# Cross attention with row sums on ScalarE, a logarithm in the row of maxima, and projections a batch sooner

## What is computed

```python
qp = q @ Wq.T
k, v = jnp.split(latent_kv @ Wkv_expand.T, 2, axis=-1)
...
scores = jnp.einsum('bhqd,bhkd->bhqk', qh, kh) * inv_sqrt_d
scores = jnp.where(causal, scores, jnp.finfo(scores.dtype).min)
attn = jax.nn.softmax(scores, axis=-1)
out = jnp.einsum('bhqk,bhkd->bhqd', attn, vh)
return out.transpose(0, 2, 1, 3).reshape(b, sq, H) @ Wout.T
```

## Time and profile before

| | us |
|---|---|
| median of 3 runs | 1062.95 |
| lowest and highest | 1061.24, 1067.86 |
| the profiled execution | 1065.82 |
| its span, first to last instruction | 1064.1 |
| cross attention within it | 293.8 to 550.7 |

### The profile page before, as it was taken

The page is one execution under the profiler, slowest core; times in us unless marked ns, Lnnn a source line. Parts: engine busy times, 40 slices in busy tenths (PEclk is TensorE's granted clock), DMA queues, the critical chain, the costliest instruction groups (busy, mean ns, idle before and its releaser), DMA issues. The chain is left out here.

```text
span 1064.1 us, 18069 instructions
## 1 busy us (share of the span) xinstructions
PE 1005.4 (94%) x6352; PEld 857.4 (81%) x6352; DVE 669.4 (63%) x1515; ACT 454.0 (43%) x803; POOL 261.4 (25%) x362
## 2 busy tenths in 40 slices
PE   7899999999979999999979989999999999999996
PEld 5688888888868888887757778989988999778785
DVE  4837546378266677776566837777777775253576
ACT  5523414236125455454534216666665664221210
POOL 4610010103143333333412012312231220503040
PEclk9999999999987999999998989999999999899999
DMA  4503013022786788877622247788778783615042
GB/s 162 194 1 119 0 59 148 0 79 97 210 224 148 218 204 233 232 218 200 212 104 73 82 144 251 246 268 279 236 263 276 253 258 110 221 36 178 19 158 79
DMA packets 87248, 172.79 MB, mean 162 GB/s; under 512 B 8113, under 2 KB 36017, under 8 KB 85393
## 3 DMA queue, kind: packets, MB, share of 16 engines
q1 hardware_dynamic: 81072, 150.21, 45.2%
q0 software_dynamic: 6112, 21.76, 6.2%
HBM read 131.05 MB, written 37.49 MB: 158 GB/s over the span
## 5 line engine op out<-in xcount | busy, mean ns | idle before, releaser
L45 PE MATMUL a_ps_proj<-region_a_rounded,arena 128*128 128x512 f32 x272 | 107.8, 396 | 10.7 <-DVE region_a_rounded L369 6.2
L45 PE MATMUL e_ps_h<-e_x_lo,e_gu_hi 128*128 128x256 f32 (+1 forms) x384 | 110.5, 288 | 3.8 <-DVE e_x_lo L2189 1.3
L962 DVE CUSTOM_DVE_ANT_0 b_dump<-b_ps_s,b_mask 128x128 f32<-128x128 f32 (+1 forms) x256 | 80.3, 353 | 48.5 <-PE b_ps_s L1157 45.3
L46 PE MATMUL e_ps_h<-e_x_hi,e_gu_lo 128*128 128x256 f32 (+1 forms) x384 | 107.5, 280 | 0.0
L47 PE MATMUL e_ps_h<-e_x_hi,e_gu_hi 128*128 128x256 f32 (+1 forms) x384 | 107.4, 280 | 0.0
L46 PE MATMUL a_ps_proj<-region_a_rounded,arena 128*128 128x512 f32 x272 | 106.7, 392 | 0.0
L47 PE MATMUL a_ps_proj<-region_a_rounded,arena 128*128 128x512 f32 x272 | 106.6, 392 | 0.0
L388 DVE SCALAR_TENSOR_TENSOR f_region_b<-a_ps_proj,a_taps,f_region_b 128x510 f32<-128x510 f32 (+2 forms) x96 | 71.7, 746 | 41.0 <-ACT f_region_b L328 38.7
L2195 DVE TENSOR_TENSOR e_gu_lo<-f_region_a,e_gu_hi 128x704 fp32r<-128x704 f32 x92 | 81.2, 886 | 16.6 <-ACT e_gu_hi L2101 16.1
L848 ACT ACTIVATE b_pt<-b_ps_x 128x384 f32<-128x384 f32 x128 | 61.8, 487 | 60.0 <-PE b_ps_x L1181 59.8
L762 POOL TENSOR_SCALAR_AFFINE_SELECT b_pt<-b_pt 128x256 f32<-128x256 f32 x128 | 54.3, 428 | 123.0 <-ACT b_pt L848 122.5
(11 more groups left out here) (418 smaller groups left out, 2665.5 us busy)
## 6 DMA issues: line engine op xcount, KB each, us to landing
f_region_a<-we_gate_up SPq DMA_DIRECT2D x88, 352.0 KB, 5.2
qk_split<-arena SPq DMA_DIRECT2D x24, 512.0 KB, 5.4
y_slots<-f_region_b SPq DMA_DIRECT2D x16, 512.0 KB, 3.7
f_x_next<-x SPq DMA_DIRECT2D x6, 1024.0 KB, 7.4
b_sk<-qk_split SPq DMA_DIRECT2D x24, 256.0 KB, 4.1
b_sq<-qk_split SPq DMA_DIRECT2D x24, 256.0 KB, 5.7
f_region_a<-we_down SPq DMA_DIRECT2D x12, 512.0 KB, 4.4
f_region_b<-we_down SPq DMA_DIRECT2D x11, 512.0 KB, 4.1
```

Of the source, the lines that this page charges most:

```text
L45: pe.matmul(out, a_hi, b_lo, start=first, stop=False)
L46: pe.matmul(out, a_lo, b_hi, start=False, stop=False)
L962: ins = dve.tensor_tensor_reduce(dump[:, n % 2, cols], ps_s[:, n % 2, cols], mask[:, cols], -1.0, 3e38, ALU.add, ALU.min, peak[:, u, k, i: ...
```

## The change

- `attend` has only its second pass; `invert`, `keep`, `spread_out`, `normalize` and `rest`, with their tiles and semaphores, are gone.
- After `maxima`, ACT takes for each head two exponentials of `dump` (128 and 256 columns; scale -1, the maximum as bias) in place, with the row sums in the accumulator output (`totals`), one head behind its `exponent`. `maxima` of a head now waits for the totals of the head two before (it writes the same `dump` buffer). Once per half ACT takes the logarithm of the sums (`logs`), DVE subtracts it from the maxima (`shifts`), and this difference goes into the rows that were those of the maxima. `maxima` scales by `SCALE`, and the row's rounding divides by it.
- ACT's table set is `natural_log_exp_and_others` instead of `exp_and_others`.
- The copies of x, queries and values move from ACT to DVE (those of the first batch's values stay). `attended` reads `ps_o`: ACT rounds directly behind `attend`, DVE subtracts at heads 0 and 1 of the next t, ahead of which POOL's `rest` was at heads 3 and 4.
- `load_peaks` moves from SP to POOL, behind the cut of head 4 of either half; the transposition moves to head 3 of either half.
- `projected(t)` is t + 3: batch 3 at t = 0, up to batch 7 at t = 4, none from t = 5. The context has three buffers (`CB`), and `split_stored` is one semaphore for each half.

```diff
...
+        CB = GB + 1
...
+        total = sb("total", [P, 2, BT, UH])
+        log_total = sb("log_total", [P, 2, BT, UH])
+        shift = sb("shift", [P, 2, BT, UH])
...
-            return {-1: GB, 0: B}.get(t, t + 2)
+            return t + 3
...
                 if b >= GB:
-                    sp.wait_ge(split_stored, split_count(b, max(u, int(b == GB))))
+                    sp.wait_ge(split_stored[u], split_count(b))
...
-            def rest(b, u):
-                pool.wait_ge(a_hi_done, 2 * b + u + 1)
-                cs = slice(UC * u, UC * u + UC)
-                pool.tensor_tensor(a_lo[:, cs], a_raw[:, cs], a_hi[:, cs].bitcast(F32), ALU.subtract).then_inc(a_lo_done, 1)
+            def load_peaks(b, u):
+                pool.wait_ge(m_lo_done, half_count(b, u))
+                for r, m in ((K_ROWS, m_hi), (K_ROWS + 1, m_lo)):
+                    pool.dma_start(sq[b % 2][r:r + 1, u].bitcast(F32), m[:, u].bitcast(F32)).then_inc(m_loaded, 16)
...
-                        if t and u == 0 and i in (3, 4):
-                            rest(t - 1, i - 3)
+                        if u == 0 and i == 4:
+                            load_peaks(t, 1)
+                        if u == 1 and i == 4 and real(t + 1):
+                            load_peaks(t + 1, 0)
...
-            act.preload_act_table_set("exp_and_others")
+            act.preload_act_table_set("natural_log_exp_and_others")
...
+                if b >= CB:
+                    act.wait_ge(v_ready, 2 * (b - CB) + 2)
+                act.activation(c_hi[:, b % CB], c_raw[:, (b % 2) * S:(b % 2 + 1) * S], ACT.Copy).then_inc(c_hi_done, 1)
...
+            def totals(b, u, i):
+                n = order(b, u, i)
+                act.wait_ge(max_done, n + 1)
+                for k, cols in ((0, slice(0, P)), (1, slice(P, 3 * P))):
+                    ins = act.activation(dump[:, n % 2, cols], dump[:, n % 2, cols], ACT.Exp, scale=-1.0,
+                                         bias=peak[:, u, k, i:i + 1], accum_out=total[:, u, k, i:i + 1])
+                ins.then_inc(total_done, 1)
+
+            def logs(b, u):
+                act.wait_ge(total_done, order(b, u, UH - 1) + 1)
+                if b:
+                    act.wait_ge(shift_done, half_count(b - 1, u))
+                act.activation(log_total[:, u], total[:, u], ACT.Ln).then_inc(log_done, 1)
...
+                    act.wait_ge(m_loaded, 32 * half_count(b - 1, u))
+                act.activation(m_hi[:, u], ps_o[0:UH, 1 - u, 0:S], ACT.Copy, scale=1.0 / SCALE).then_inc(m_hi_done, 1)
...
-            def keep(b):
-                act.wait_ge(rinv_lo_done, inverse_count(b))
-                if b:
-                    act.wait_ge(spread_ready, 2 * b)
-                act.activation(r_hi[:], rinv[:], ACT.Copy).then_inc(r_hi_o_kept, 1)
...
             def attended(b, u):
-                act.wait_ge(a_raw_done, 2 * b + u + 1)
+                act.wait_ge(o_ready, half_count(b, u))
                 if b:
                     act.wait_ge(out_ready, 2 * b)
-                cs = slice(UC * u, UC * u + UC)
-                act.activation(a_hi[:, cs], a_raw[:, cs], ACT.Copy).then_inc(a_hi_done, 1)
-
-            values(0, 0)
-            values(0, 1)
+                act.activation(a_hi[:, UC * u:UC * u + UC].rearrange("p c t -> p (c t)"), ps_o[:, u], ACT.Copy)\
+                    .then_inc(a_hi_done, 1)
...
+                        if i == 0 and (u == 0 or real(t + 1)):
+                            totals(t + u, 1 - u, UH - 1)
+                            logs(t + u, 1 - u)
+                        if i and real(t + 1):
+                            totals(t + 1, u, i - 1)
                         fill(t, u, i)
-                        if i == 4 and u == 0:
+                        if i == 3 and u == 0:
                             peaks(t, 1)
-                        if i == 1 and u == 1 and real(t + 1):
+                        if i == 3 and u == 1 and real(t + 1):
                             peaks(t + 1, 0)
-                        if t >= 1 and u == 0 and i in (2, 3):
-                            attended(t - 1, i - 2)
...
-                keep(t)
-            for u in range(2):
-                attended(B - 1, u)
+                for u in range(2):
+                    attended(t, u)
...
             def turned(b, u):
-                dve.wait_ge(xkq_hi_done, x_count(b, u))
+                dve.wait_ge(xkq_ready, x_count(b, u))
+                if b > GB:
+                    dve.wait_ge(xkq_ready, q_count(b - 1, 1))
                 cs = slice(UC * u, UC * u + UC)
-                dve.tensor_tensor(x_lo[:, cs].rearrange("p c t -> p (c t)"), ps_pj[:, u],
-                                  x_hi[:, cs].rearrange("p c t -> p (c t)").bitcast(F32), ALU.subtract).then_inc(xkq_lo_done, 1)
+                hi, lo = (x[:, cs].rearrange("p c t -> p (c t)") for x in (x_hi, x_lo))
+                dve.tensor_copy(hi, ps_pj[:, u]).then_inc(xq_hi_done, 1)
+                dve.wait_ge(xq_hi_done, x_hi_count(b, u))
+                dve.tensor_tensor(lo, ps_pj[:, u], hi.bitcast(F32), ALU.subtract).then_inc(xkq_lo_done, 1)
...
+                dve.wait_ge(xkq_ready, q_count(b, u))
+                hi, lo = (split[:, u, k].rearrange("p c t -> p (c t)") for k in (QH, QL))
+                dve.tensor_copy(hi, ps_pj[:, 1]).then_inc(xq_hi_done, 1)
+                dve.wait_ge(xq_hi_done, q_hi_count(b, u))
+                dve.tensor_tensor(lo, ps_pj[:, 1], hi.bitcast(F32), ALU.subtract).then_inc(xkq_lo_done, 1)
+
+            def values(b, k):
+                dve.wait_ge(v_ready, 2 * b + k + 1)
+                if b >= 2:
+                    dve.wait_ge(o_ready, half_count(b - 2, 1))
+                dve.tensor_copy(v[:, b % 2, k], ps_pj[:, k]).then_inc(v_done, 1)
+
+            def shifts(b, u):
+                dve.wait_ge(log_done, half_count(b, u))
+                if b:
+                    dve.wait_ge(m_ready, half_count(b - 1, u))
+                dve.tensor_tensor(shift[:, u], peak[:, u], log_total[:, u], ALU.subtract).then_inc(shift_done, 1)
 
             def peaks(b, u):
-                dve.wait_ge(m_hi_done, 2 * b + u + 1)
-                dve.tensor_tensor(m_lo[:, u], ps_o[0:UH, 1 - u, 0:S], m_hi[:, u].bitcast(F32), ALU.subtract)\
-                    .then_inc(m_lo_done, 1)
+                dve.wait_ge(m_hi_done, half_count(b, u))
+                dve.scalar_tensor_tensor(m_lo[:, u], ps_o[0:UH, 1 - u, 0:S], 1.0 / SCALE, m_hi[:, u].bitcast(F32),
+                                         ALU.mult, ALU.subtract).then_inc(m_lo_done, 1)
+
+            def attended(b, u):
+                dve.wait_ge(a_hi_done, half_count(b, u))
+                hi, lo = (x[:, UC * u:UC * u + UC].rearrange("p c t -> p (c t)") for x in (a_hi, a_lo))
+                dve.tensor_tensor(lo, ps_o[:, u], hi.bitcast(F32), ALU.subtract).then_inc(a_lo_done, 1)
...
-                    dve.wait_ge(max_done, n - 1)
+                    dve.wait_ge(total_done, n - 1)
                 dve.wait_ge(s_ready, n + 1)
                 for k, cols in ((0, slice(0, P)), (1, slice(P, 3 * P))):
                     ins = dve.tensor_tensor_reduce(dump[:, n % 2, cols], ps_s[:, n % 2, cols], mask[:, cols],
-                                                   -1.0, 3e38, ALU.add, ALU.min, peak[:, u, k, i:i + 1])
+                                                   -SCALE, 3e38, ALU.add, ALU.min, peak[:, u, k, i:i + 1])
                 ins.then_inc(max_done, 1)
...
+                        values(t + 1, i - 5)
...
+                        if t >= 1 and u == 0 and i < 2:
+                            attended(t - 1, i)
+                        if u == 0 and i == 1:
+                            shifts(t, 1)
+                        if u == 0 and i == 4:
                             peaks(t, 1)
-                        if u == 1 and i == 2 and real(t + 1):
+                        if u == 1 and i == 1 and real(t + 1):
+                            shifts(t + 1, 0)
+                        if u == 1 and i == 4 and real(t + 1):
                             peaks(t + 1, 0)
...
-                pe.wait_ge(max_done, order(b, u, UH - 1) + 1)
+                pe.wait_ge(shift_done, half_count(b, u))
                 t = b if u == 1 else b - 1
                 if t >= 1:
-                    pe.wait_ge(a_raw_done, 2 * (t - 1) + (1 if u == 1 else 2))
+                    pe.wait_ge(a_lo_done, half_count(t - 1, 1 - u))
                 for r in range(BT):
-                    mm = pe.transpose(ps_o[0:UH, 1 - u, r * P:(r + 1) * P], peak[:, u, r], ident[:])
+                    mm = pe.transpose(ps_o[0:UH, 1 - u, r * P:(r + 1) * P], shift[:, u, r], ident[:])
...
-                pe.wait_ge(exp_done, HEADS * (b + 1) - 1)
+                pe.wait_ge(v_done, 2 * b + 2)
                 for c in range(DC):
                     pe.wait_ge(cut_done, HEADS * b + HC * (c + 1))
-                    for r in range(BT):
-                        for h in range(HC):
```

(17 more changed lines are left out.)

206 lines of the change are left out of this document (62 added, 144 removed).

## The result

| | before | changed |
|---|---|---|
| median (lowest to highest) | 1064.08 us (1059.04 to 1067.86), 20 runs | 1068.37 us (1062.74 to 1073.49), 20 runs |
| ratio, 95% interval | | 1.0038, 1.0021 to 1.0055 |
| the profiled execution, its span | 1065.82, 1064.1 | 1070.3, 1068.3 |
| PE, DVE, ACT busy | 1005, 669, 454 | 984, 679, 532 |

The change costs 4 us. 1068 lies in the predicted range and within 1% of before, but on the other side of it than the 1058 forecast. PE is busy for 21 us less and the kernel takes longer.

The account below looks back on a forecast made before the run. PE was taken to set the pace in t = 1 to 4. The terms 1 + 9.5 - 6.5 - 3.3 - 2.2 - 3.5 sum to -5.0 from the runs' median 1062.95, giving 1058 us; range 1042 to 1075.

Parts of the forecast that it names:

- The start: Ahead of t = 0: two x copies in series on DVE and keys behind the first row of maxima on ACT, +1 us.
- t = 0: First batch, now projecting batch 3: ACT needs 25 us, low clock could make it 31; taken as 28, +9.5 on 18.5.
- What ACT gets: ACT's two exponentials per head with accumulator reads: 0.85 us per head, the read taken as 0.08.
- Rival D: ACT's accumulator read costs 0.23 us instead of 0.08, 4.8 us more per batch: 1072 us, chance 0.06.
- F: Rival: each logarithm swaps ACT's table there and back, 41 us, three quarters on the path: 1089 us, chance 0.03.
- t = 1 to 4: Four full batches: sum pass gone, DVE late for the queries (PE stands 2.3 us), 1.5 us gained each, -6.5 together.
- rival C: PE's clock falls in every batch after the hole before the queries, two query units costing 1.35 us more each: 1077, chance 0.14.
- t = 5 and 6: Batches without projections: between 23.6 us by ACT's load and 29 at low clock, taken as 26.5 each, -3.3 together.
- Rival B: Engines overlap well and the clock holds: t = 1 to 4 at 27.2, t = 5 and 6 at 23.6; 1043 us, chance 0.26.
- t = 7: Last batch: loses the sum pass (2.67 us), 0.5 given back for its row of maxima, -2.2.
- Rival E: The rows of maxima land late, in 6 us, costing 1.8 in each of eight batches: 1072 us, chance 0.06.
- The tail: From the last attend to the last projection: 5.1 us instead of 8.6, -3.5.

Follow-up runs that it names:

- e4: Changed kernel with the row sums left out: each ACT exponential covers one column without accumulator, so it computes something else; 1066.36 us, 1.0022 of before.
- e1: Changed kernel with DVE's order changed at a batch's start: shifts' subtraction directly behind head 1's maxima, outputs' subtractions at heads 1 and 2; 1066.33 us, 1.0034 of before.
- e5: e1 plus two orders: ACT rounds the context ahead of head 0's row sums, PE transposes the shifts behind head 3's query projection; 1063.23 us, 1.0003 of before.

## Why the prediction was wrong

**The start (+1, was +4.5).** I counted x's two copies and the keys behind the maxima, not that on ACT the row sums stand ahead of the values, the context and the keys' second half. PE's waits there: 0.54, 1.10, 2.17 and 2.88, where before has none, 0.72, 1.23 and 1.78; and 0.86 and 1.47 for maxima, for none and 0.74. A size, from an order that was in the diff to be read.

**t = 0 (+9.5, was +9.2).** The number is right, with ACT at 24.2 busy and the clock at 0.71. The reason is not ACT's load, from which I had 25: in e4 ACT is busy 18.0 us there and t = 0 takes 26.1, in e1 24.0 us and it takes 26.0. PE is busy for 24.9 of the 27.7 us at its low clock, and that sets the length for the most part.

**What ACT gets (0.85 per head, is 0.88).** Right. ACT's groups in the stage:

```profile
L798 ACT ACTIVATE b_dump<-b_dump,b_peak 128x256 f32<-128x256 f32 x128 | 63.7, 498 | 0.0
...
L798 ACT ACTIVATE b_dump<-b_dump,b_peak 128x128 f32<-128x128 f32 x128 | 50.4, 394 | 14.6 <-DVE b_peak L941 14.5
L798 ACT ACTIVATION_READ_ACCUMULATOR b_dump<-b_dump,b_peak 128x1 f32 x256 | 48.9, 191 | 0.0
```

The read of the accumulator lasts 0.19, but the next instruction starts 0.09 after it does: 386.69 to 387.57 for one head's two exponentials and reads. Rival D, a read of 0.23 that counts in full, is out; so is F, as no table is loaded between the exponentials and the logarithms.

**t = 1 to 4 (-6.5, was +5.2): the step that failed.** I had DVE late at the batch's start, as it is, but for one reader only, the queries' wait for x, and put the hole at 2.3 us with the clock at 1.00. I forecast 1.5 us gained in each and 1.2 were lost (31.35 for 30.2 in t = 3). Three things in it are wrong. First, the place: the shifts' transposition stands on PE ahead of the query, and what it needs stands on DVE behind x and the outputs; and the context stands on ACT behind row sums and a logarithm. I costed the logarithm and the subtraction by their own length and for the row's landing, not by who queues behind them. The queries begin 9.6 to 9.7 us after the attend where my working gives 8.8 and before had 10.1. Second, the second half: the value waits 0.84 for the query's low part, not 0.3. Third, the clock, which I gave to rival C with 0.14: one spell, 1.5 us, in three of the batches and two in the other. For t = 3 that is 0.8 + 0.5 + 1.5 = 2.8 against the 2.7 between forecast and result. e5 shows what the order was worth: with it mended t = 2 to 4 keep their clock and take 28.8 us, and the total falls by 3.5 us.

**Rival C**'s mechanism is what happened in t = 1 to 4, at less than its price: 1.5 for each spell, not 2.7, since a spell ends within the query units, and not in the rest, as t = 0 came out at 28 and t = 5 and 6 at 24. The Trainium skill (TensorE: Matmul & The Clock Gate, HAM oscillation) has dense work broken by waits start slow each time, in a kernel whose waits are longer than the 2.3 us of my working; "by it C is what happens" went further than the page. The trace agrees in the changed kernel's every batch, and disagrees in e1's and e4's t = 2, where the same holes as in their t = 3 left the clock at 1.00.

**t = 5 and 6 (-3.3, was -8.3).** I took 26.5 each between 23.6 and 29; they are 24.0, ACT busy 21.6 and 22.3 as worked out (21.5). Rival B's number for this part, 23.6, was the better one; I had it and let the clock outweigh it. That it came from ACT's load is not borne out: in e4 ACT is busy 15.5 and 15.6 us there, and the two take 24.4 and 24.1, with a spell more each.

**t = 7 (-2.2, was +1.4).** Rival E, in this batch: 3.97 us for the row, which took 5.7 to land. The others hide it but for 0.6 us in t = 1, at 1.7 to 1.9 us of landing in the median, half of the 3.5 I took.

**The tail (-3.5, was -4.4).** Right: attend at 545.51, the last projection at 549.76, 4.25 us for 5.1.

**Behind the stage (0, was -3.5 in the profile).** I took the program that does not change to take a time that does not change. The profiles show it does not, by 3 to 7 us: 11.3 and 11.1 us of clock are lost there in before, 5.1 and 4.9 in the changed kernel, and the work is the same. As far as the profiles go, that is why a stage that ends 7.7 and 8.0 us later costs 4 us. Both profiles of before have less clock than its median execution, so part of this may be those two executions.

**The sum.** That 1068 lies in the range is luck in part. The start, t = 1 to 4 and t = 7 came out 3.5, 11.7 and 3.6 us worse than forecast, t = 5 and 6 and the tail 5.0 and 0.9 better, and the part behind the stage 3.5 better.

## What to carry to other kernels

An operation that moves to another engine takes a place in its queue, and a small one (here a subtraction of 0.17 us) can be worth ten times its length to whoever waits behind what stands ahead of it: write out both queues around it, instruction by instruction, before adding up lengths. The same work in another order was worth 7 us here and turned the change from 0.36% slower into 0.3% faster. An engine with idle time in the middle of a batch could take more here (ACT went from 15 to 24.5 us busy of 30 without setting the pace); what stood ahead of its first results after the batch's start was paid for. When a wait is taken away by delaying something else, look for every in-order queue in which that something is awaited: here three in a row had to be mended before the gain was seen in the stage.

## What the runs showed of the hardware

- PE's clock fell in spells that lose 1.7 us each, or 3.4 where two follow; the profiled executions lose 23 to 33 us of clock in all, some 8 of them in the thinly fed t = 0 of before. Two executions of one kernel have them in the same places in t = 1 to 6 and not everywhere in t = 0 and 7; a batch with the same holes a few us earlier or later need not have them (e1 and e4, t = 2 against t = 3). A part that was not edited took 506.5 to 513.6 us in the nineteen profiles. The Trainium skill (TensorE: Matmul & The Clock Gate, The HAM clock gate) says that the gate watches on its own time, which does not start with the kernel, and that the point of warm-up varies between runs of one kernel for it. The trace agrees between kernels. Between executions of one, the two profiled ones differ by a spell or two, and the mean clock of whole executions ranges from 0.966 to 0.975 in the changed kernel and from 0.975 to 0.986 in before.
- Behind the stage such spells came and went with 5.6 us of PE's busy time (485.6 and 480.0 for the same matmuls), 0.5% of this kernel, in a part that no edit touched: a profile's stage and the kernel's total are two different answers at this size.
- ACT's accumulator read: 0.19 us by itself, 0.09 in the queue. DVE's rounding copy from PSUM, 128x512: 0.68 to 0.69, where ACT's takes 0.58 to 0.59.
- An 8 KB transfer of GpSimd's queue: two to issue in 1.05 us of its queue, landed in 1.7 to 1.9 in the median and in 5.1 to 5.7 beside SP's large transfers.
